# Key rows from digit rows on TensorE, attribute rows in quarters, zeroing issued first: a graph kernel on one Trainium2 core

## Time and profile before

| what | value |
|---|---|
| median of 3 runs | 3574.64 us (3573.5 to 3580.78) |
| the profiled execution: its time | 3583.88 us |
| the profiled execution: its span | 3582.1 us |
| mean granted TensorE clock | 0.93 |
| busy: PE, DVE, ACT, POOL | 82%, 78%, 64%, 59% of the span |
| moved by DMA | 422.8 MB, mean 118 GB/s |
| stage 0, in the profile | 27 to about 900 us |
| stage 1 | 1114 to 2920 us |

### The profile page before, as it was taken

How to read it: one execution, slowest core, us unless ns; L and a number is a source line. 1 busy time by engine, 2 the same in 40 slices (tenths; PEclk the granted TensorE clock), 3 DMA queues, 4 the chain that set the end, 5 groups by cost and what they waited for, 6 DMA issues and landing times. The chain is left out here.

```text
span 3582.1 us, 70126 instructions
## 1 busy us (share of the span) xinstructions
PE 2928.3 (82%) x19604; PEld 2347.2 (66%) x19605; DVE 2801.5 (78%) x6559; ACT 2302.2 (64%) x3192; POOL 2110.6 (59%) x1633
## 2 busy tenths in 40 slices
PE   5877888888304999999999999999999976557656
PEld 4876787787203888888888888888888851113256
DVE  8879888888204999999999999999999983341054
ACT  6876888888203888888888888888888842230000
POOL 4017777777777777777777777777777740000000
PEclk9998999999556999999999999999999988788878
DMA  9973333333322222222222322232223259998830
GB/s 388 422 285 35 45 47 44 50 44 36 28 1 25 51 52 49 50 51 51 51 49 51 51 52 49 50 50 51 51 49 50 51 169 427 426 416 350 361 157 5
DMA packets 258165, 422.78 MB, mean 118 GB/s; under 512 B 149095, under 2 KB 174312, under 8 KB 251576
## 3 DMA queue, kind: packets, MB, share of 16 engines
q0 software_dynamic: 149536, 124.64, 19.9%
q1 hardware_dynamic: 92152, 224.49, 18.0%
q10 hardware_dynamic: 16416, 72.92, 5.0%
HBM read 290.44 MB, written 131.45 MB: 118 GB/s over the span
## 5 line engine op out<-in xcount | busy, mean ns | idle before, releaser
L557 POOL DMA_INDIRECT both<-kept x784 | 1279.0, 1631 | 547.1 <-issue 235.8
L888 PEld LDWEIGHTS ps<-prod,big 128*128 128x128 f32 x7840 | 1135.3, 190 | 179.5 <-DVE prod L1242 174.5
L888 PE MATMUL ps<-prod,big 128*128 128x170 f32 x7840 | 1185.3, 311 | 60.1 <-DVE prod L1242 60.0
L565 POOL DMA_INDIRECT kept<-feat_dram,kept x784 | 786.8, 1004 | 262.8 <-issue 178.3
L639 ACT ACTIVATE big<-iota_b,kept 128x640 f32<-128x640 f32 x1029 | 779.2, 815 | 13.6
L879 PE MATMUL ps<-prod,onehot 128*128 128x320 f32 x3920 | 671.6, 321 | 101.5 <-DVE prod L1273 76.7
L879 PEld LDWEIGHTS ps<-prod,onehot 128*128 128x128 f32 x3920 | 586.1, 190 | 117.7 <-DVE prod L1273 100.5
L644 ACT ACTIVATE big<-big 128x2560 f32<-128x2560 f32 x196 | 458.0, 2337 | 317.8 <-PE ps L888 317.7
L949 PE MATMUL ps<-w2mix,kept 65*128 65x384 f32 x1568 | 559.3, 500 | 21.7 <-ACT kept L691 20.4
L1413 DVE TENSOR_REDUCE kept<-kept 128x80 f32<-128x1280 f32 x392 | 561.2, 1470 | 0.0
L949 PEld LDWEIGHTS ps<-w2mix,kept 65*128 65x128 f32 x1568 | 284.1, 191 | 179.7 <-issue 25.5
(11 more groups left out here) (220 smaller groups left out, 2789.2 us busy)
## 6 DMA issues: line engine op xcount, KB each, us to landing
both<-big POOLq DMA_DIRECT2D x40, 2000.0 KB, 104.8
big<-both SPq DMA_DIRECT2D x50, 1600.0 KB, 10.6
adj_w<-kept ACTq DMA_DIRECT2D x32, 800.0 KB, 32.9
big<-adj_w SPq DMA_DIRECT2D x32, 800.0 KB, 12.4
big<-adj_w ACTq DMA_DIRECT2D x32, 800.0 KB, 11.8
kept<-keys_dram SPq DMA_DIRECT2D x98, 256.0 KB, 3.5
kept<-keys_dram SPq DMA_DIRECT2D x196, 128.0 KB, 2.9
kept<-in_wT SPq DMA_DIRECT2D x196, 128.0 KB, 2.8
```

The source lines that it names most:

```text
L557: pool.indirect_dma_start(both, bass.IndirectOffsetOnAxis(ap=sc_idx[:, c:c + 1], axis=0), sc_val[:, c // 2, c % 2, :], None, compute_op=AL ...
L565: pool.indirect_dma_start(gath[:, s % 2, k, :], None, feat_dram, bass.IndirectOffsetOnAxis(ap=src_i[:, 4 * s + k:4 * s + k + 1], axis=0)). ...
L888: mm = pe.matmul(part_sums(part, MSG), onehot[:, q, k, part * P:(part + 1) * P], prod[:, q, k, 0:HI * MSG], start=False, stop=False, skip_ ...
```

## The change

1. **Key rows.** DVE also makes the turned keys as integers, cuts them into three digits (bits 16 and up, 8 to 15, 0 to 7) and converts them to bf16; SP stores the three digit rows to `parts_dram`. A group's load is now 3 rows of 512 bf16 (3 KB). PE multiplies them with `places`, a [3, 128] matrix of 65536, 256 and 1, into PSUM bank 7 (`spread_keys`), and `compare_group` on ACT reads the row from there. Stage 1 keeps its broadcast loads.
2. **Attributes** come in four loads of 64 KB every four steps, each waiting for its own step.
3. **Zeroing.** POOL sets only the first 2400 columns of `zeros`, drops the three waits for inputs, issues the small store and four of the 40 pieces, makes the constants, then issues the rest.
4. **Edge layout.** The host now cuts the edges in order: partition p of chunk c is edge 128 c + p. The padding fills chunks 782 and 783 and part of 781; POOL leaves out the gathers and scatters of 782 and 783 (USED = 782).

```diff
+USED = -(-EDGES // P)
-        keyrow = edge(2, 4 * P)
+        keyrow = edge(2, 2 * P)
+        keyp = edge(2, 4 * P, dt=BF16, parts=3)
 @block.sync
-            sp.wait_ge(s_keysd, 16)
+            for t in range(3):
+                sp.dma_start(parts_dram[t:t + 1, :].rearrange("o (q j) -> (o q) j", q=112), digit[:, t, :]).then_inc(s_keysd, 16)
+            sp.wait_ge(s_keysd, 64)
             def load_group(g, slot):
                 if not first(g):
-                    sp.wait_ge(s_gap, 6 * (g - 1))
-                load_keys(4 * g, 4, slot)
+                    sp.wait_ge(s_rowps, g - 1)
+                sp.dma_start(keyp[:, slot, :], parts_dram[:, ds(g * (4 * P), 4 * P)]).then_inc(s_keyp[slot], 16)
             def load0(u):
-                load_group(u * 2, 0)
-                load_attr(u)
-                load_group(u * 2 + 1, 1)
+                for k4 in range(4):
+                    if k4 % 2 == 0:
+                        load_group(u * 2 + k4 // 2, k4 // 2)
+                    if not first(u, 1):
+                        if k4 == 0:
+                            sp.wait_ge(s_rows, u)
+                        else:
+                            sp.wait_ge(s_prod[0], u * 16 + (4 * k4 - 16))
+                    load_attr(u * 4 + k4, k4)
 @block.gpsimd
-            pool.memset(zeros, 0.0).then_inc(s_zero, 1)
...
+            pool.memset(zeros[:, 0:NA * ROW], 0.0).then_inc(s_zero, 1)
             pool.wait_ge(s_zero, 1)
-            pool.wait_ge(s_in["idxT"], 32)
-            pool.wait_ge(s_in["idx"], 32)
-            pool.wait_ge(s_in["w"], 16)
...
+                if t == 3:
+                    setup_tiles()
...
-                    gather(s + 1, range(4))
+                    gather(s + 1, range(min(4, USED - 4 * (s + 1))))
                 if s >= BEHIND:
-                    for c in range(2):
-                        add(2 * (STEPS + s - BEHIND) + c)
+                    for c in range(2 * (STEPS + s - BEHIND), min(2 * (STEPS + s - BEHIND) + 2, USED)):
+                        add(c)
 @block.scalar, compare_group
-                act.wait_ge(s_krow[slot], g * 8 - slot * 8 + 16)
+                act.wait_ge(s_rowps, g + 1)
-                    act.activation(key_gap[:, lo * P:(lo + n) * P], keyrow[:, slot, col * P:(col + n) * P], ACT.Square,
+                    act.activation(key_gap[:, lo * P:(lo + n) * P], ps[:, 7, col * P:(col + n) * P], ACT.Square,
 @block.tensor
+            def spread_keys(g, slot):
+                pe.wait_ge(s_keyp[slot], 8 * (g - slot) + 16)
+                if not first(g, 1):
+                    pe.wait_ge(s_gap, 6 * g)
+                pe.matmul(ps[:, 7, :], places[:, :], keyp[:, slot, :], start=True, stop=True).then_inc(s_rowps, 1)
 phase0, after merge_open
+                if k4 % 2 and not is_last(s, 4):
+                    spread_keys(g + 1, 1 - slot)
 @block.vector
+            link(V.scalar_tensor_tensor(out=keyT_i, in0=srcT, scalar=float(NP), in1=dstT, op0=ALU.mult, op1=ALU.add))
+            V.tensor_scalar(digit_i[:, 0, :], keyT_i, 16, None, ALU.arith_shift_right)
+            V.tensor_scalar(digit_i[:, 1, :], keyT_i, 8, 255, ALU.arith_shift_right, ALU.bitwise_and)
+            link(V.tensor_scalar(digit_i[:, 2, :], keyT_i, 255, None, ALU.bitwise_and))
+            V.tensor_copy(digit, digit_i).then_inc(s_keyT, 1)
...
-                dve.wait_ge(s_gath[q], 64 * (t + 1))
+                dve.wait_ge(s_gath[q], 64 * (t + 1) - (16 * (CH - USED) if is_last(s) else 0))
 the host
-    src, dst = (padded(i[k], CH * P, NP - 1).reshape(P, CH) for k in ("src", "dst"))
+    def chunks(name, fill):
+        a = padded(i[name], CH * P, fill)
+        return a.reshape((CH, P) + a.shape[1:]).swapaxes(0, 1).reshape(P, -1)
+    src, dst = (chunks(k, NP - 1) for k in ("src", "dst"))
```

More of the change, by code:

```diff
@@ L237, in gnn_program @@
         onehot = rings[:, 4 * 640:12 * 640].rearrange("p (q k n) -> p q k n", q=2, k=4)
+        keyT_i = rings[0:112, 0:7 * P].bitcast(I32)
+        digit_i = rings[0:112, 7 * P:28 * P].bitcast(I32).rearrange("p (t n) -> p t n", t=3)
+        digit = rings[0:112, 28 * P:28 * P + 21 * P // 2].bitcast(BF16).rearrange("p (t n) -> p t n", t=3)
         tmp_i = big[:, 3, 0:CH].bitcast(I32)
@@ L268, in gnn_program @@
         s_rlen = sem("rel_len_ready")
+        s_keyp = [sem(f"key_parts{q}") for q in range(2)]
+        s_rowps = sem("group_keys_in_psum")
         s_krow = [sem(f"keyrow{q}") for q in range(2)]
@@ L399, in _, with load_keys, load_attr @@
             sp.dma_start(keys_dram.rearrange("(q j) p -> q (j p)", j=7), keyT).then_inc(s_keysd, 16)
-            sp.wait_ge(s_keysd, 16)
-            def load_keys(first_c, n, q):
-                row = keys_dram[ds(first_c, n), :].rearrange("(o c) p -> o (c p)", o=1)
-                sp.dma_start(keyrow[:, q, 0:n * P], row.broadcast_to([P, n * P])).then_inc(s_krow[q], 16)
+            for t in range(3):
+                sp.dma_start(parts_dram[t:t + 1, :].rearrange("o (q j) -> (o q) j", q=112), digit[:, t, :]).then_inc(s_keysd, 16)
+            sp.wait_ge(s_keysd, 64)
+            def load_keys(d, q):
+                row = keys_dram[ds(2 * d, 2), :].rearrange("(o c) p -> o (c p)", o=1)
+                sp.dma_start(keyrow[:, q, :], row.broadcast_to([P, 2 * P])).then_inc(s_krow[q], 16)
             def load_group(g, slot):
                 if not first(g):
-                    sp.wait_ge(s_gap, 6 * (g - 1))
-                load_keys(4 * g, 4, slot)
[L413 to L418, removed]
-            def load0(u):
-                load_group(u * 2, 0)
-                load_attr(u)
-                load_group(u * 2 + 1, 1)
+                    sp.wait_ge(s_rowps, g - 1)
+                sp.dma_start(keyp[:, slot, :], parts_dram[:, ds(g * (4 * P), 4 * P)]).then_inc(s_keyp[slot], 16)
+            def load_attr(s, k4):
+                sp.dma_start(attr[:, 4 * k4:4 * k4 + 4, :].rearrange("p k f -> p (k f)"),
+                             ea32_in[:, ds(s * (4 * FEAT), 4 * FEAT)]).then_inc(s_attr, 16)
+            def load0(u):
+                for k4 in range(4):
[7 more added lines that the diff above has]
+                    load_attr(u * 4 + k4, k4)
             load0(0)
@@ L438, in load1 @@
             def load1(s, q, t):
-                sp.wait_ge(s_gap, 6 * GROUPS0 + 2 * (s - 1) if not first(s) else 6 * (GROUPS0 - 1 + s))
-                load_keys(2 * (s + STEPS), 2, q)
+                if not first(s):
+                    sp.wait_ge(s_gap, 6 * GROUPS0 + 2 * (s - 1))
+                load_keys(s + STEPS, q)
                 if not first(s):
@@ L513, in _ @@
         def _(pool):
-            pool.memset(zeros, 0.0).then_inc(s_zero, 1)
[L515 to L537, removed]
+            def setup_tiles():
+                pool.memset(ident[:, :], 0.0).then_inc(s_const, 1)
+                pool.memset(earlier[:, :], 1.0).then_inc(s_const, 1)
+                pool.memset(valid[:, :], 1.0).then_inc(s_const, 1)
+                pool.wait_ge(s_const, 3)
+                pool.affine_select(out=ident[:, :], in_=ident[:, :], compare_op=ALU.not_equal, fill=1.0,
+                                   base=0, pattern=[[-1, P]], channel_multiplier=1).then_inc(s_const, 1)
+                pool.affine_select(out=earlier[:, :], in_=earlier[:, :], compare_op=ALU.is_gt, fill=0.0,
+                                   base=0, pattern=[[1, P]], channel_multiplier=-1).then_inc(s_const, 1)
+                pool.affine_select(out=valid[:, :], in_=valid[:, :], compare_op=ALU.is_gt, fill=0.0,
+                                   base=NODES, pattern=[[-P, NA]], channel_multiplier=-1).then_inc(s_const, 1)
+                pool.iota(iota_b[:, :], [[1, PARTS * P]], base=0, channel_multiplier=0,
+                          allow_small_or_imprecise_dtypes=True).then_inc(s_const, 1)
+                pool.iota(iota_a[:, :], [[1, HI]], base=0, channel_multiplier=0,
+                          allow_small_or_imprecise_dtypes=True).then_inc(s_const, 1)
+                pool.iota(spare[:, :], [[P, 4]], base=BIG, channel_multiplier=1,
+                          allow_small_or_imprecise_dtypes=True).then_inc(s_const, 1)
+                pool.iota(node_ids[:, :, 0], [[P, NA]], base=0, channel_multiplier=0,
+                          allow_small_or_imprecise_dtypes=True).then_inc(s_const, 1)
+                pool.iota(node_ids[:, :, 1], [[0, NA]], base=0, channel_multiplier=1,
+                          allow_small_or_imprecise_dtypes=True).then_inc(s_const, 1)
@@ L909, in phase0 @@
                     merge_hop(g, slot, 1)
+            spread_keys(0, 0)
+            spread_keys(1, 1)
             merge_open(0, 0)
@@ L1172, in _ @@
             dve.wait_ge(s_in["idxT"], 32)
-            V.scalar_tensor_tensor(out=keyT, in0=srcT, scalar=float(NP), in1=dstT,
-                                   op0=ALU.mult, op1=ALU.add).then_inc(s_keyT, 1)
+            V.scalar_tensor_tensor(out=keyT, in0=srcT, scalar=float(NP), in1=dstT, op0=ALU.mult, op1=ALU.add)
```

(18 more changed lines are left out.)

12 lines of the change are left out of this document (8 added, 4 removed).

## The result

The changed kernel takes 3522.9 us (median of 4 runs), the kernel before 3576.3 beside it: a ratio of 0.9857, 95% interval 0.9833 to 0.9881. That is 53 us off where 66 were forecast, and 14.9 us above the 3508 given, well inside the range. The profiled execution has a span of 3533.1 us, for 3582.1 before.

What follows compares the result with a forecast made beforehand. Bound: zeroing, then 392 scatters, then the first gather. Start 221, clash 5, 325 scatters at 2.12 us and 67 in 133 us put the gather at 1048 for 1114.27: -66 us from 3574.6, so 3508 us, range 3474 to 3565.

Steps and rivals of the forecast that it cites:

- The bound: Start of stage 1: end of zeroing at 243.26 us plus 392 scatters, with the first gather queued behind them on POOL.
- The start: First scatter near 221 us, -22: zeroing issued 6 earlier, key loads 16, digit rows -1.5, straggling engine 1.5.
- The straggler: One DMA engine finishing late at the zeroing's end, 27 GB/s from 234 to 236 us; 1.5 us off was taken.
- The clash: Loads of x and edge_attr_3, before under the zeroing, now meet the first scatters: +5 us (0 to 12).
- Landing excess: POOL's waits in stage 0 for earlier scatters to land, above plain issue time: 73 us, of which 18 would stay.
- The first rival: All landing excess vanishes: -86 us, 3489, first gather at 1028; chance 0.13.
- the rival by number of loads: Only the start moves; landing waits stay because they count loads, not bytes: -13 us, 3562; chance 0.12.
- The cover: The table, ready 174 us before the first gather, hides extra PE, ACT and DVE time in stage 0.
- the worst case: Added stage 0 delays at most: DVE's start 10, PE's matmuls 37, attribute quarters 44 us; table at about 1031.
- signs of being wrong: Wrong if scatter spacing is 2.3 or more, DVE's single wait is gone, or PE idles behind the spread.
- The term taken as fixed: POOL's scatter instruction in stage 0, 1.70 us, within the spacing 1.70 + 0.353 + 18/284 = 2.12 us.
- Slower by the order of edges: Rival: 128 neighbours in dst order make memory serve scatters slower; at 0.6 us each, 3626; chance 0.07.

Runs made afterwards that it cites:

- e4: The kernel before with only POOL's start reordered so that the zeroing is issued first; ratio to the kernel before 0.9985.
- e3: The changed kernel with key rows loaded broadcast to 128 partitions as before, no digits and no spread; 3617.8 us, ratio to the kernel before 1.0094.
- e7: The changed kernel with the spread matmul at the head of PE's step and attributes in one load; ratio to the kernel before 0.9854.
- e2: The changed kernel with the attributes in one load of 256 KB for 16 chunks, as before; ratio to the kernel before 0.9849.
- e1: The changed kernel with the spread matmul moved on PE to the head of the same step, ahead of its four sums; ratio to the kernel before 0.9845.
- e5: The kernel before with the changed edge order alone (chunks of 128 neighbours); ratio to the kernel before 0.9998.
- e6: The changed kernel with the edge order of before and no chunk left out; ratio to the kernel before 0.9843.
- e8: e7 with the edge order of before and no chunk left out; ratio to the kernel before 0.9852.

## Why the prediction was right, and where it was wrong

- **The bound.** Right as a start: zeroing, then 392 scatters, then the gather. The time moved by what the first gather moved, 53 us. In the changed kernel, though, the gather waits for the table and no longer for the scatters.
- **The number is in part luck.** The scatters ended at 1022.4, 26 us ahead of the 1048 forecast, and the wait for the table put 39 us on top. Two misses of opposite sign left 13 us.
- **The start.** -22 was forecast, -21.9 measured, but the terms are not those of the sum. The earlier zeroing was to give 6 us, "partly shared", and gave 3.0 (e4); the key loads were to give 16 and gave 10.3 (e3 against the changed kernel); 8.6 came with e3's other changes, which no term held. With attributes whole and stage 0 at full pace (e7) the start is 226.2, -17, and 225.2 with whole attributes alone (e2): some 4 to 5 of the 22 us are owed to the quarters, and the fit is luck. The straggler stayed, 25 to 28 GB/s from 213 to 219 us.
- **The clash.** +5 was charged; none shows. With stage 0 slow under the zeroing, pass 13 and x's load moved from 221 to 291 us, and the landing waits there stayed within the few left.
- **Landing excess.** 18 us left of 73 was forecast. 7.9 - 6 x 0.343 = 5.8 us are left. The first rival, all gone, was the truth for POOL: its sum put the gather at 1028, and the scatters were done at 1022.4. e2 and e3 show that the broadcast key loads, 16 packets an engine in every four steps, made the waits; the rival by number of loads, with 4 quarters for 1, fell. The rule of the Trainium skill ("DMA: Bandwidth & Descriptors", "Queues, rings and completion order") on turns between queues was worked out there to keep the waits; the 7.9 us left don't bear that out.
- **The cover: the step that failed.** "No new stall, and ACT needs it two steps later" was argued from the merge's input. It overlooked that ACT had been running ahead of PE and lived on that lead. The spread stands behind PE's sums, those wait for ACT's one-hots, and ACT may start them only after the compare that waits for the spread: a ring through two queues, with 159 us of waits, and PE idle enough to lose some of its clock. It costs 71 to 85 us of stage 0 (e1 against the changed kernel, e2 against e7). The quarters, at 44 us in the worst case, cost 31 to 45 (e2 against the changed kernel, e1 against e7), of which 29.8 us are DVE's nine waits for attributes. PE's matmuls (up to 37) and DVE's start (up to 10) show no cost. In all 1054.7 - 938.8 = 116 us against 91 for the worst case, while the scatters' end came 92 us nearer: the cover of 174 us was used up. Of the prediction's own signs of being wrong one came true, PE standing idle around the spread, and another nearly did: DVE's single wait fell to 13.8 us, where about 95 was forecast.
- **The term taken as fixed.** POOL's own 1.70 us went into the sum unchanged. It depends on what DVE does at that moment: 1.66 with a slowed stage 0, 1.78 at full pace. This, and not the cover, decides the time: with the cover whole the ratio is 0.9845 (e1) or 0.9854 (e7), and the gather starts at 1056 in both, 8 us after the forecast 1048. The prediction's spacing of 2.12 would then have been nearly right (2.14 in e1, 680.0 us for 318 scatters), with a longer instruction and less waiting than its terms say.
- **A slip in the sums.** 80 scatter rows ahead, used at 2.12 and made at 2.4 us a row, last 1450 us and not 1300; nothing hangs on it.
- **Slower by the order of edges.** Fell: e5 0.9998, e6 and e8 like their partners. **Padding** 0, as said.

Left open: why scatters start later in a product pass in the kernel before than in e7 and e3, which is what makes their instruction 1.68 us there and 1.76 and 1.81 here. A landing wait may shift them; no run tests it. Nor does any run separate the quarters from the edge order and the earlier zeroing in e3.

## What to carry to other kernels

When a slack is spent as cover, follow each new handoff around its whole ring: which queue gives, which takes, and what the giver itself is waiting for; an engine that ran ahead of another loses that lead the moment it must wait for it. Measure the cover with the change's own delays, for a gain large enough uses it up; and when the slow part is made quick again, measure the other side anew, for it may depend on it. Where POOL's indirect DMAs set the pace, try cutting DVE's long two-input passes short, even at the price of more DVE time; here it gave 0.8%.

## What the runs showed that I had not expected

An indirect scatter of 128 rows that starts inside a two-input DVE pass of 1.49 us is held to its end, up to 1.13 us more in the rows shown; the mean instruction ranged from 1.610 to 1.807 us by what else ran. And with PE standing some 2 us idle before its sums, again and again, the granted clock had a mean of 0.89 from 400 to 800 us; in e1, the same kernel without these waits, it was 1.00, as in the kernel before.
